# Attention scores in tiles of 64 rows by 32 columns

## The reference

```python
q, k = ...  # (B, 32, T, 8) each;  v: (B, 16, T, 16)
scores = jnp.einsum('bhtd,bhsd->bhts', q * scaling, k)
attn_w = softmax(scores)
aw = attn_w.reshape(B, 16, 2, T, T)
aw = aw[:, :, 0] - lam * aw[:, :, 1]
attn = jnp.einsum('bhts,bhsd->bhtd', aw, v)
```

## Time and profile before

| | |
|---|---|
| median of 3 runs | 4305.11 us (4297.64 to 4307.68) |
| profiled execution, span | 4305.0 us |
| mean granted clock of PE | 0.967 |
| PE busy | 3865.9 us, 90% |
| ACT busy | 3799.3 us, 88% |
| DVE, POOL busy | 1213.6 us (28%), 629.2 us (15%) |
| loads and matmuls on PE | 26194 of each |

### The profile page before, as it was taken

How to read it: one execution, slowest core, us unless ns; L and a number is a source line. 1 busy time by engine, 2 the same in 40 slices (tenths; PEclk the granted TensorE clock), 3 DMA queues, 4 the chain that set the end, 5 groups by cost and what they waited for, 6 DMA issues and landing times.

```text
span 4305.0 us, 79997 instructions
## 1 busy us (share of the span) xinstructions
PE 3865.9 (90%) x26194; PEld 933.8 (22%) x26194; DVE 1213.6 (28%) x2854; ACT 3799.3 (88%) x4132; POOL 629.2 (15%) x401
## 2 busy tenths in 40 slices
PE   5698998989899898999979999898998989999996
PEld 2121211212122121221212222121221212212123
DVE  7321212223232222223332232222331212112124
ACT  1599998989889998998989999898998999999992
POOL 4110212111020110202102020110200101010100
PEclk8799999999999999999999999999999999999998
DMA  3302112210231212112130121212212120221201
GB/s 120 79 24 34 42 29 35 37 29 27 33 50 33 51 32 38 42 33 48 33 47 30 33 48 33 51 28 39 45 25 44 24 38 6 32 27 28 34 13 58
DMA packets 112652, 165.25 MB, mean 38 GB/s; under 512 B 18820, under 2 KB 86660, under 8 KB 111880
## 3 DMA queue, kind: packets, MB, share of 16 engines
q1 hardware_dynamic: 112072, 158.19, 19.6%
HBM read 97.82 MB, written 60.32 MB: 37 GB/s over the span
## 4 chain that ended last, share of the span: by engine, by line
issue 74%; ACT 9%; PE 7%; POOL 6%; DVE 2%; ACTq 1%; DMA 0%; POOLq 0%; DVEq 0%; SPq 0%
ACT probs L597 9%; POOL seg_rs L570 4%; PE ps L642 2%; PE ps L715 2%; PE ps L702 1%; ACTq L594 1%; DVE a_qk L915 0%; DVE normed L830 0%; PE ps L617 0%; POOL a_rest L531 0%; POOL a_parts L533 0%; POOL e_rstd L547 0%; POOL a_rstd L521 0%; DMA m_scr<-wmod_sb 0%; DVE c_exp L843 0%
## 5 line engine op out<-in xcount | busy, mean ns | idle before, releaser
L597 ACT ACTIVATE probs<-ps 128x1024 f32<-128x1024 f32 x4096 | 3778.0, 1259 | 331.5 <-PE ps L702 331.1
L715 PE MATMUL ps<-probs,values 128*32 128x512 f32 x16384 | 2209.3, 612 | 6.4 <-DVE seg_t L958 6.2
L702 PE MATMUL ps<-queries,keys 64*128 64x512 bf16 x8192 | 1533.2, 390 | 301.4 <-issue 83.0
L702 PEld LDWEIGHTS ps<-queries,keys 64*128 64x128 bf16 x8192 | 367.4, 93 | 2418.8 <-ACT probs L597 2258.1
L570 POOL TENSOR_TENSOR seg_rs<-seg_ms,neg_half 64x16 f32<-64x16 f32 x128 | 370.2, 2892 | 2770.9 <-DVE seg_ms L967 2770.9
L958 DVE STREAM_TRANSPOSE seg_t<-ps 128x512 f32<-128x512 f32 x128 | 91.8, 717 | 1316.1 <-PE ps L715 1314.8
L715 PEld LDWEIGHTS ps<-probs,values 128*32 128x32 f32 x16384 | 324.0, 108 | 568.6 <-issue 506.7
L969 DVE TENSOR_TENSOR seg_n<-seg_d,seg_rs 64x256 f32<-64x256 f32 x128 | 53.4, 417 | 384.6 <-POOL seg_rs L570 384.6
L941 DVE TENSOR_TENSOR e_tmp<-ps,e_gate 128x512 f32<-128x512 f32 x64 | 44.2, 691 | 352.5 <-PE ps L624 351.2
L915 DVE TENSOR_SCALAR a_qk<-ps 128x512 f32<-128x512 f32 x64 | 44.3, 691 | 339.8 <-PE ps L642 336.0
L973 DVE SCALAR_TENSOR_TENSOR seg_a<-seg_n,subln_sb 32x256 f32<-32x256 f32 x256 | 105.7, 413 | 6.0
(11 more groups left out here) (119 smaller groups left out, 1260.2 us busy)
## 6 DMA issues: line engine op xcount, KB each, us to landing
queries<-q_scr SPq DMA_DIRECT2D x384, 64.0 KB
keys<-k_scr SPq DMA_DIRECT2D x384, 64.0 KB
v_scr<-a_v SPq DMA_DIRECT2D x128, 128.0 KB, 1.8
values<-v_scr SPq DMA_DIRECT2D x32, 512.0 KB
q_scr<-a_parts SPq DMA_DIRECT2D x32, 384.0 KB, 2.6
k_scr<-a_parts SPq DMA_DIRECT2D x32, 384.0 KB, 2.5
a_x<-in_x_dram SPq DMA_DIRECT2D x16, 512.0 KB, 3.9
attn_scr<-seg_o SPq DMA_DIRECT2D x128, 64.0 KB, 1.6
```

What stands on the lines that cost most here:

```text
L597: nc.scalar.activation(probs[:, u % PRING, n % PAIRS, :, :], slots[slot_of(n)], ACT.Exp).then_inc(exp_done, 1)
L702: last = nc.tensor.matmul(slots[slot_of(n)][:, half, :], keys[buf][at:at + KS_ROWS, n % PAIRS, blk * P:(blk + 1) * P], queries[buf][at:at ...
L715: last = nc.tensor.matmul(pv[j:j + VW, :], values[buf][:, blk, half, :], probs[:, u % PRING, pair, half, :], start=(blk == 0), stop=(blk = ...
```

## The change

The scores of one n for 128 keys come from eight matmuls instead of two. Each half's 128 keys are cut into four times 32; the load of the stationary operand takes 32 columns, and the result goes to 32 rows of the same bank. The streamed operand, 64 rows by 512 queries, is the same for all four. The results lie where they lay before. The wait for exponential n - 3, and the one for a group's loads at units 0 and 64, become lone waits on PE. Only the last matmul raises `scores_ready`, as before.

```diff
             def scores(body, u, n):
 
                 buf, tc, blk = u // UNITS, u // NB % NC, u % NB
-                pe.wait_ge(exp_done, body * (2 * BODY) + n + 1 + (n in (1, 2 * BODY - 1)))
+                wait_alone(pe, exp_done, body * (2 * BODY) + n + 1 + (n in (1, 2 * BODY - 1)), pe_passed)
                 for half in range(2):
                     at = 64 * half
-                    last = nc.tensor.matmul(slots[slot_of(n)][:, half, :], keys[buf][at:at + KS_ROWS, n % PAIRS, blk * P:(blk + 1) * P],
-                                            queries[buf][at:at + KS_ROWS, n % PAIRS, tc * CH:(tc + 1) * CH], start=True, stop=True)
+                    for j in range(0, P, 32):
+                        k0 = blk * P + j
+                        last = nc.tensor.matmul(slots[slot_of(n)][j:j + 32, half, :], keys[buf][at:at + KS_ROWS, n % PAIRS, k0:k0 + 32],
+                                                queries[buf][at:at + KS_ROWS, n % PAIRS, tc * CH:(tc + 1) * CH], start=True, stop=True)
                 last.then_inc(scores_ready, 1)
...
                         if u % UNITS == 0:
                             buf = u // UNITS
-                            pe.wait_ge(group_loaded[buf], (body + 1) * (GROUP_LOADS * DMA))
+                            wait_alone(pe, group_loaded[buf], (body + 1) * (GROUP_LOADS * DMA), pe_passed)
```

## The result

The changed kernel takes 4456.97 us (median of 4 runs, 4430.27 to 4483.78) against 4306.1 us (median of 4 runs, one more than in the table of before): a ratio of 1.0355, 95% interval 1.0313 to 1.0398. It is 151 us slower where 34 were forecast. Its runs also spread over 54 us, those of the kernel before over 10. The profiled execution has a span of 4482.0 us, the longest of the four, 177 us over the 4305.0 of before. Lines of the file are 17 to 19 lower than before: the exponential is L578, the scores L685, the weighted sum L698.

What follows compares the result with a forecast made beforehand. ACT was taken to lead most of the time, with PE deciding in some 205 places. Steps 30 + 1 and loop heads 3 gave 34 us onto 4305.0: 4339, forecast 4340, range 4300 to 4395 (the forecast's own 4316 to 4375).

Steps and rivals of the forecast that it cites:

- PE decides: ACT's waits for the scores: about 206 to 240 of them, with 331 + 35 us.
- the undisturbed unit: Two heads, 128 keys, at ACT's rate: stays at 1.83 us, so the added PE time is covered, cost 0.
- A pair: Load and matmul of a score tile: 7 ns each, 0.044 us more for each head.
- PE behind: PE's unit when it lags, scores to scores: 1.53 us rises to 1.62, still under 1.83.
- the lower figure named beside my own: Score tiles: about 4 ns for each further tile by the skill, giving 4332 us in place of 4340.
- switch: Change of tiling between scores and weighted sum costs about 0.10 us; 0 gained, as a bound 0.10 each side.
- D: Rival, scores next to weighted sum: switch costs no drain; with a free lone wait 23 us faster, 4282 us; 5%.
- The steps: Other work put into PE's units: about 157 waits, each 0.19 us longer, 30 us, plus 1 for short steps.
- the full 0.19: PE's lateness per unit: 0.10 us for the lone wait plus 2 x 0.044 for the tiles.
- the lone wait: Wait for the exponential as its own instruction: 0.10 us, bounds 0 and 0.12, counting only for the second head.
- The heads: Start of the loop's body, 16 of them: 0.2 us each, 3 us.
- rival B: PE's code arrives too late, at the block after the loop's head: 16 x 2.8 = 45 us, 4385 us; 8%.

Runs made afterwards that it cites:

- waits_only: The kernel before with only the lone waits, its two 64 x 128 matmuls a head kept: 4323.68 us, ratio 1.0045.
- tiles_away: The changed kernel with 32-column tiles only outside the units in which a group is loaded, lone waits everywhere: 4357.59 us.
- short_loads: The changed kernel with a group's query and key rows loaded only to 64 of 2048 columns: 4337.2 us; the kernel before, cut likewise, 4301.25 us.
- tiles_during: The changed kernel with 32-column tiles only inside the units in which a group is loaded, lone waits everywhere: 4464.75 us.
- code_in_loads: The kernel before with 8 waits for a raised semaphore behind the weighted sum, only in the units of the loads, no tiles: 4328.71 us.
- tiles_64: The changed kernel with tiles of 64 x 64, four matmuls a head in place of eight: 4355.44 us, ratio 1.0123.
- code_longer: The kernel before with 16 increments of an unused semaphore on PE behind each unit's weighted sum: 6251.52 us, ratio 1.4526.
- code_longer_waits: The kernel before with 16 waits for a raised semaphore on PE behind each unit's weighted sum: 4916.19 us, ratio 1.1415.

## Why the prediction was wrong

**What held.** ACT leads, PE decides in 238 places (206 to 240 forecast), and the undisturbed unit stays at 1.83 us: all as forecast. The tiles run at once. A pair costs 3 ns, not the 7 that I took from the weighted sum, and PE behind needs 1.55 us, not 1.62. Here the lower figure named beside my own was right: the Trainium skill (TensorE: Matmul & The Clock Gate, Part 3) gives about 4 ns for each further tile, and by that rule the trace agrees. The scores start 0.07 us before the modelled end of a weighted sum (1850.80 + 1.07 against 1851.80), and the weighted sum 0.07 before that of the scores (1851.80 + 0.91 against 1852.64), as in the kernel before (0.06 and 0.07). So no switch was saved, and D is out. The steps were to give 30 + 1 us; the table shows 152.0 + 38.9 against 138.0 + 38.6, 14 us, as the full 0.19 was paid at few of them: a step that costs 1.49 in place of 1.33 pays 0.16, and by the same count those at units 26 and 106 pay less than 0.1. Of the 14 us the lone wait has 8. The heads were to give 3 us and gave 9, since each was cut inside its first scores: one matmul, 2.14 us of nothing, then fifteen, as the timeline of PE at the head shows:

```profile
402.16 0.58 PE L685 MATMUL ps<-queries,keys 64*32 64x512 bf16 x1 [3.28 <-issue]
404.89 1.05 PE L685 MATMUL ps<-queries,keys 64*32 64x512 bf16 x15 [2.14 <-issue]
405.87 1.93 PE L698 MATMUL ps<-probs,values 128*32 128x512 f32 x8
```

With units 10 to 12, behind the head, it is 16 us. So without late blocks the change would have cost 31 us in the profiled execution (178 less 147), where 34 were forecast; but that the two agree is luck, since the steps came to 14 in place of 31 and the heads to 16 in place of 3.

**The step that failed** is in rival B, code that arrives too late: 8%, and 45 us if it came. I looked for it at the wrong place (the block after the head) and excluded it elsewhere with two sentences: in straight code no gap shows, and a block's units take 8 us where its fetch takes 3. The 3 us had been read at a head, where little else moves on the DMA engines. In units 13 to 22 their share is 0.69 to 1.03 and in 88 to 99 0.46 to 0.95 (means of bodies 1 to 11 of the kernel before). There the fetch of a block waits among the data, and PE went on 10.6 to 19.9 us after the block before had begun, where the prediction had 3 us for a fetch and 8 for a block. The kernel before has 28 instructions a unit and 256 in a block: 256 / 28 x 1.83 = 17 us of time for each fetch. The change has 54: 8.7 us. That no gap showed in straight code before meant that 17 us were enough where its blocks happened to fall, not that 8.7 would be: with 30 instructions a unit, blocks of 15.7 to 17.5 us came late once in waits_only and six times in tiles_away. The column that would have told this is in the same view of windows by which I added up ACT's idle time: the share of the DMA engines, but in windows of 10 us and not of a body, where it is 0.16.

**How sure.** That the loss needs the data of the loads is shown by short_loads (151 down to 36 us), that it needs the long code in just those units by tiles_during and tiles_away, and that the stands are late blocks by the table of landings: each of the 43 ends behind a landing of PE's code. That length alone does it, without tiles, rests on code_in_loads, in which nine such stands with some 18 us appear, and on tiles_64 between; the two runs meant to show it at full size failed, so the full 115 to 147 us without tiles are not shown. The sizes agree only roughly: the medians give 115 us for what goes with the data, the profiled execution, the longest of the four, 147 for late blocks. The DMA engines need not all be full: from the begin of the block before to the late packet's start their mean share was 0.89 to 1.07 at eight of the nine stands of unit 19, but 0.47 to 0.53 at the four of unit 92. Which transfers a block's fetch stands behind, and why PE stands 1 us in one body and 10.6 in another, stays open. The spread of the runs fits it, but isn't explained by it.

## What to carry to other kernels

A change that costs an engine no time can still cost it code. Count the instructions of a unit before and after, divide 256 by them, and compare the time of a block with the longest fetch while the DMA engines are busy (some 20 us here, by the table of landings), not with the fetch in a quiet stretch. Where an engine's program is long and has loops, look at the heads for standstills that wait for nothing: here 16 instructions ahead of a loop gave 0.6%, and they with the loop written out two bodies at a time 1.4%.

## What the runs showed of the hardware

PE's code comes in blocks of 16 KB (281 packets of 4.60 MB, 489 of 8.01). A block holds 256 instructions: code_longer adds 16 x 2048 = 32768 of them and its page shows 409 blocks, 128 more. The Trainium skill (Runtime: NRT & Kernel Launch, Instruction fetch mechanics) describes such blocks of 256 and calls the cost of crossing from one to the next mostly hidden. The trace agrees with the size; as to the cost the measurement decides, and up to 10.6 us stood open inside a head.

An instruction of PE that only waits for a raised semaphore takes its sequencer 0.106 us, and one that increments a semaphore 0.151 (code_longer_waits and code_longer, from one to the next). Pairs of load and matmul that are already waiting start 0.003 us apart; what they cost the sequencer the trace doesn't show. I had counted 0.05 from the length that the trace gives such an instruction by itself.

Eight matmuls of 64 rows by 32 columns on eight places of the array take as long as two of 64 by 128, within 0.02 us a head (0.63 us for two heads against 0.61).

After a stand of 10.6 us PE's granted clock was 0.50, the lower of its two levels, until 3414, 5.5 us after it went on; ahead of the stand it was 1.00.
